# A decoder block on one core: x transposed before the third weight piece, the last batch's norms by token half, its natural scores on four strips

## The reference, cut to what matters

```
A:  qkv = bitlinear(x)            # x rounded to 8 bits per token, weights replaced by their sign
    local softmax over 16 heads of one token; + q @ kv_state of the first 128 tokens
    x1 = layernorm(x + bitlinear(rmsnorm(out)))
B:  q = [ctx, x1] @ Wq ; two key/value sources, one from ctx and one from x1, 32 heads of 16
    scores + alibi, only the last 64 keys ("window"), softmax over both sources
    x2 = layernorm(x1 + att @ Wo)
C:  router over 8 experts, the best two, LoRA weights scaled by them
    y = layernorm(x2 + x2 @ base_w.T + b + lora)
```

## Time and profile before

| | |
|---|---|
| time, median of 3 runs (lowest, highest) | 913.03 us (912.97, 913.53) |
| the profiled execution's own time | 913.3 us |
| its span, first to last instruction | 911.2 us |
| PE, busy share | 802.1 us, 88% |
| DVE | 509.5 us, 56% |
| ACT | 326.4 us, 36% |
| POOL | 85.5 us, 9% |

### The profile page before, as it was taken

The page is one execution under the profiler, slowest core; times in us unless marked ns, Lnnn a source line. Parts: engine busy times, 40 slices in busy tenths (PEclk is TensorE's granted clock), DMA queues, the critical chain, the costliest instruction groups (busy, mean ns, idle before and its releaser), DMA issues.

```text
span 911.2 us, 22548 instructions
## 1 busy us (share of the span) xinstructions
PE 802.1 (88%) x10161; PEld 524.5 (58%) x10209; DVE 509.5 (56%) x1060; ACT 326.4 (36%) x424; POOL 85.5 (9%) x103
## 2 busy tenths in 40 slices
PE   3788878888998989988998989988998979999996
PEld 2466763477445864577445864577445864486443
DVE  4756584448745593748745593648745582435143
ACT  5534224333245224433245224433245124310422
POOL 1111011000300021000300021000300010010001
PEclk9989999999999999999999999999999999997998
DMA  9921000100002000010002000010001000000000
GB/s 345 246 55 47 2 2 1 47 2 2 2 1 70 3 2 1 26 47 2 1 1 71 3 2 1 27 46 1 1 1 48 2 1 1 24 1 1 1 24 23
DMA packets 19022, 27.10 MB, mean 30 GB/s; under 512 B 5608, under 2 KB 7784, under 8 KB 18928
## 3 DMA queue, kind: packets, MB, share of 16 engines
q1 hardware_dynamic: 18784, 25.64, 9.1%
q10 hardware_dynamic: 144, 0.03, 0.0%
HBM read 21.47 MB, written 4.19 MB: 28 GB/s over the span
## 4 chain that ended last, share of the span: by engine, by line
PE 63%; DVE 19%; ACT 12%; issue 4%; POOL 1%; DMA 1%; ACTq 0%; POOLq 0%; SPq 0%; DVEq 0%
ACT p_b L761 7%; PE ps L1148 7%; PE ps L1184 6%; PE ps L1065 6%; PE ps L1225 6%; DVE max_b L1487 6%; PE ps L1113 4%; PE ps L1048 3%; PE ps L1085 3%; PE ps L893 2%; DVE max_a L1385 2%; PE ps L968 2%; PE ps L1173 2%; PE ps L1157 2%; PE ps L978 2%
## 5 line engine op out<-in xcount | busy, mean ns | idle before, releaser
L761 ACT ACTIVATE p_b<-ps 128x2048 f32<-128x2048 f32 x64 | 106.5, 1664 | 115.9 <-PE ps L1157 115.9
L1487 DVE TENSOR_REDUCE max_b<-ps 128x4 f32<-128x768 f32 (+2 forms) x160 | 106.6, 711 | 31.1 <-PE ps L1127 19.3
L1363 DVE SCALAR_TENSOR_TENSOR nat<-ps,st_a,qkv_bias 128x512 f32<-128x512 f32 x48 | 35.7, 744 | 98.0 <-PE ps L893 96.8
L1113 PE MATMUL ps<-qk_b 32*128 32x192 f32 (+2 forms) x1024 | 65.5, 341 | 22.9 <-DVE max_b L1487 16.8
L1148 PE MATMUL ps<-qk_b 32*128 32x512 f32 (+1 forms) x512 | 66.2, 586 | 9.7 <-ACT p_b L761 5.2
L1113 PEld LDWEIGHTS ps<-qk_b 32*128 32x128 f32 x1024 | 46.2, 188 | 39.9 <-DVE max_b L1487 27.3
L1225 PE MATMUL ps<-base_t,x_t 128*128 128x512 f32 x128 | 63.8, 624 | 0.0
L1173 PE MATMUL ps<-p_b,v_b 128*32 128x256 f32 (+1 forms) x1024 | 61.7, 358 | 2.4 <-ACT p_b L761 2.0
L1048 PE MATMUL ps<-c_t,wq 128*128 128x256 f32 x256 | 60.6, 385 | 2.4 <-DVE out_a L1408 2.3
L1065 PE MATMUL ps<-x_t,wq 128*128 128x256 f32 x256 | 61.3, 385 | 0.0
L1184 PE MATMUL ps<-wo,o_fb 128*128 128x512 f32 x128 | 59.0, 599 | 0.8 <-DVE o_fb L1529 0.8
(11 more groups left out here) (207 smaller groups left out, 1432.7 us busy)
## 6 DMA issues: line engine op xcount, KB each, us to landing
x_in<-x SPq DMA_DIRECT2D x8, 512.0 KB, 5.4
p_b<-ctx SPq DMA_DIRECT2D x8, 512.0 KB, 4.6
y<-x SPq DMA_DIRECT2D x7, 512.0 KB, 3.3
p_b<-L_attn_qkv_w SPq DMA_DIRECT2D x2, 1024.0 KB, 6.5
p_b<-L_xattn_Wq SPq DMA_DIRECT2D x1, 2048.0 KB, 14.9
x<-L_attn_qkv_w SPq DMA_DIRECT2D x2, 512.0 KB, 9.5
x<-L_ffn_base_w SPq DMA_DIRECT2D x2, 512.0 KB, 10.2
wo<-L_xattn_Wo SPq DMA_DIRECT2D x8, 128.0 KB, 9.1
```

The lines of the kernel that those rows point to most:

```text
L761: act.activation(p_b[:, j % 2, :, 0:cols], ps[:, 4:8, 0:cols], ACT.Exp, scale=DB ** -0.5).then_inc(pb_here.sem, 1)
L1113: pe.matmul(bank(4 + r)[:, (i % 2) * N:(i % 2) * N + 2 * n * S], q_b[strip[r], i, :, :].rearrange("p h q -> p (h q)"), k_b[strip[r], half, ...
L1363: dve.scalar_tensor_tensor(nat[:, t, w, :], bank(nat_bank(b, w)), st_a[:, 2, t:t + 1], qkv_bias[:, w * C:(w + 1) * C], ALU.mult, ALU.add). ...
L1487: ins = dve.tensor_reduce(max_b[:, half, 0, i:i + k, 2 * n:2 * n + 2], ps[:, 4 + 2 * n:6 + 2 * n, :].rearrange("p r (i n) -> p i r n", i=2 ...
```

## The change

What is the same for all batches: in `b2`, the scores of the even query block on strips 0 and 1 are issued after DVE's first report of the pair before, those on strips 2 and 3 after the second, then the odd block's on all four; slopes and masks go to strips 0 and 1 for both blocks, and then to strips 2 and 3.

```
+                if pair:
+                    sb_max(pe, b, 8 * half + 2 * pair - 1)
+                scores(even, first)
+                if pair:
                     sb_max(pe, b, 8 * half + 2 * pair)
...
+                scores(even, second)
+                scores(odd, first)
+                scores(odd, second)
+                for strips in (first, second):
+                    slope(even, strips)
+                    slope(odd, strips)
+                    masks(even, strips)
+                    masks(odd, strips)
```

```
             def b2(b, half, pair):
-                alone = isinstance(b, int) and b == NB - 1
+                keep_on(b, NB - 1, (0, 0, 6, 6, 4, 4, 2, 2)[4 * half + pair])
...
             def c1_x2(b, t):
-                    keep_on(b, NB - 1, 2 if t else 14)
+                    keep_on(b, NB - 1, 4)
                     x2_here(pe, b, t + 1)
-                    if t:
+                    if alone(b):
+                        pb_here(pe, b)
+                    elif t:
...
             def c1(b, t):
                 keep_on(b, NB - 1, 2)
-                x2t_here(pe, b)
+                if alone(b):
+                    outa_here(pe, b)
+                x2t_here(pe, b, t + 1 if alone(b) else None)
...
+            def half_stats(c, b, t, z, mv, rs, row, here):
+                c.start(dve, b, 2 * t)
+                c.link(dve.bn_stats(stats[:, t, :], z[:, t, :]))
+                c.link(dve.bn_aggr(mv[:, t, :], stats[:, t, :]))
+                dve.tensor_scalar(rs[:, row, t:t + 1], mv[:, t, 1:2], EPS_LN, None, ALU.add).then_inc(here.sem, 1)
+
+            def half_shift(b, t, mv, rs, row, rstd, done):
+                rstd(dve, b, t + 1)
+                dve.scalar_tensor_tensor(rs[:, row + 2, t:t + 1], mv[:, t, 0:1], -1.0, rs[:, row + 1, t:t + 1], ALU.mult, ALU.mult).then_inc(done.sem, 1)
```

```
+            def warm(n):
+                for _ in range(n):
+                    pe.matmul(bank(7).rearrange("p (a n) -> p a n", a=4), eyeb, eyeb.unsqueeze(1).to_broadcast([P, 4, P]), start=True, stop=True)
+
             for n in range(2):
+                warm((22, 3)[n])
                 pe.wait_ge(signed.sem, n + 1)
                 sign_turn(n)
...
             def early(b):
+                warm(3)
...
             def a1(b):
+                if isinstance(b, int) and b == 0:
+                    warm(11)
...
-            first = [(0, late), (1, mix), (0, b1), (1, a0), (2, a0), (1, b1)]
+            first = [(0, late), (0, b1), (1, b1), (1, a0), (2, a0), (1, mix)]
...
-            first = [(-1, early), (0, a1), (0, of(a1_qkv, 0, [0])), (0, of(a1_qkv, 0, [1])), (0, of(a1_qkv, 0, [2])), (0, of(a1_qkv, 1, [0])),
+            first = [(0, a1), (-1, early), (0, of(a1_qkv, 0, [0])), (0, of(a1_qkv, 0, [1])), (0, of(a1_qkv, 0, [2])), (0, of(a1_qkv, 1, [0])),
```

More of the change, by code:

```diff
@@ L411, in program, with alone @@
         NEXT, A, B, C_, D_ = -1, 0, 1, 2, 3
+        def alone(b):
+            return isinstance(b, int) and b == NB - 1
         def apart(b, t):
@@ L575, in b4 @@
             def b4(b):
+                if alone(b):
+                    for t in range(T):
+                        vb_here(pool, b, t + 1)
+                        pool.tensor_tensor(rs_b[:, 1, t:t + 1], rs_b[:, 0, t:t + 1], neghalf[:, 0:1], ALU.pow).then_inc(rb_here.sem, 1)
+                    return
                 vb_here(pool, b)
@@ L1100, in b2 @@
                         v_here(pe, b)
-                        if not alone:
+                        if not (isinstance(b, int) and b + 1 >= NB):
                             ct_here(pe, b + 1)
-                elif not alone:
-                    sb_max(pe, b, 8 * half + 2 * pair)
-                seen = [(i, slice(max(i - 2, 0), i + 1)) for i in (2 * pair, 2 * pair + 1)]
-                o = lambda r, i, n: bank(4 + r)[:, (i % 2) * N:(i % 2) * N + 2 * n * S].rearrange("p (c k) -> p c k", c=n)
@@ new lines, in b2, with scores @@
+                cols = lambda i: slice((i % 2) * N, (i % 2) * N + 2 * S * (min(i, 2) + 1))
+                keys = lambda i: slice(max(i - 2, 0), i + 1)
+                first, second = range(2), range(2, 4)
+                def scores(i, strips):
+                    for r in strips:
+                        pe.matmul(bank(4 + r)[:, cols(i)], q_b[strip[r], i, :, :].rearrange("p h q -> p (h q)"),
+                                  k_b[strip[r], half, keys(i), :, :].rearrange("p c s k -> p (c s k)"),
+                                  start=(i % 2 == 0), stop=False, skip_group_check=True)
@@ new lines, in slope, with masks @@
+                def slope(i, strips):
+                    for r in strips:
+                        at = slice(r * S, r * S + 3)
+                        pe.matmul(bank(4 + r)[:, cols(i)], slopes[at, half, :], places[at, keys(i), :], start=False, stop=False, skip_group_check=True)
+                def masks(i, strips):
+                    for r in strips:
+                        o = bank(4 + r)[:, cols(i)].rearrange("p (c k) -> p c k", c=min(i, 2) + 1)
+                        if i < 2:
+                            mm = pe.matmul(o[:, i, :], rep[strip[r], :], mask_nat[strip[r], 1, :], start=False, stop=True, skip_group_check=True)
+                        else:
+                            mm = pe.matmul(o[:, 0:3:2, :], rep[strip[r], :], mask_nat[strip[r], :, :], start=False, stop=True, skip_group_check=True)
+                        if i % 2 and r % 2:
+                            mm.then_inc(sb_full.sem, 1)
```

202 lines of the change are left out of this document (100 added, 102 removed).

## The result

The changed kernel took 904.2 us (903.5 to 905.2, 4 runs) where the one before took 913.0 in the same comparison (911.2 to 913.5): ratio 0.9894, interval 0.9874 to 0.9914. The chain has the same shape, but TensorE waits far less for VectorE's maxima in the natural scores. The page's chain after, then the views of waits before (L1113 is the scores' product) and after (L1130): us in total, times, longest.

The account below looks back on a forecast made before the run. PE was taken as the main bound, with 63% of the chain of waits. Terms -4.3 -0.5 +2.4 -0.8 -0.5 -2.6 -3.1 sum to -9.4 from 913.3, giving 904.0 us after adjustment; 8-in-10 range 899.5 to 910.5.

Parts of the forecast that it names:

- the +2.4 of the body: Body's natural scores: two-strip groups cost 0.46 us in each of five iterations, rounded up to +2.4.
- Start-up: 22 identity products raise PE's clock and x is transposed before the third weight piece: -4.3 us at batch 0's last block.
- The rival with the signs held up: Start-up: the 22 products delay the sign transposes, gaining 1 instead of 4.3 us; 907.3 us, chance 0.13.
- Slopes and masks of strips 0 and 1, then of 2 and 3, no longer share the array four at a time: Natural scores, batches 0 to 6: the second group of slopes and masks costs 0.23 us a pair, 0.14 in pairs 0 and 4.
- Batches 0 and 6: Natural scores where DVE and PE alternate: about five pairs on the path save 0.15 us each, -0.8 in all.
- Batch 7's scores: Natural scores on four strips with identity products: the low clock goes and maxima are transposed earlier, -2.6 us.
- The +4.2: Batch 7's scores at full clock: period 2.97 against 2.25 on two strips, six pairs losing 0.7 us each.
- The end: Batch 7's last norms by halves: -2.6 us up to the router, -0.5 in the last norm, -3.1 in all.
- (1): Rival: the clock falls in batch 7's scores all the same, -2.6 becoming +2.4; 908.9 us, chance 0.15.
- (2): Rival: two-strip groups are paid in full in all 56 pairs, +12.9 instead of +1.6; 915.2 us, chance 0.11.
- (3): Rival: the 22 start-up products hold up the signs, gaining 1 instead of 4.3 us; 907.3 us, chance 0.13.
- (4): Rival: reorderings of `first` and `last` bring 3 us more than seen; 901 us, chance 0.11.

Follow-up runs that it names:

- e6: Changed kernel without its 39 start-up identity products, x still transposed ahead of the third weight piece; 902.5 us.
- e2: Changed kernel with 3, 4, 3 and 4 identity products ahead of the pairs of batch 0's second half of natural scores; 904.4 us.
- e1: Changed kernel with natural scores of batches 0 to 6 on four strips as before, batch 7 keeping two-strip groups; 906.6 us.
- e3: Changed kernel with batch 7's two last layer norms taken over both token halves at once, as before; 910.0 us.
- e5: Changed kernel run again with no edit, to see differences between executions; 903.1 us.
- e9: Changed kernel with 12 start-up identity products for 22, batch 7's scores two strips at a time again, no products ahead of its pairs; 909.6 us.
- e12: Changed kernel with 12 start-up identity products for 22, plus 4 at 38 us in TensorE's wait for ACT's maxima copy; 898.8 us.
- e4: Changed kernel without the 24 identity products ahead of batch 7's pairs of natural scores; 907.6 us.
- e10: As e9, but with 16 identity products ahead of batch 7's two-strip groups; 909.3 us.
- e11: Changed kernel with 12 start-up identity products for 22, batch 6's last base quarter back behind batch 7's first transposed scores; 903.2 us.

## Why the prediction was right, and where it was not

904.0 was said and 904.2 measured. The direction and the large terms were right, but that the sum fits this well is luck, since its errors cancel: the +2.4 of the body did not come, the start-up and batch 7's transposed scores gained 1.9 more than was said, the end 0.7 more, and against them stood 3.5 in batch 0 that was not foreseen and about 1.8 of small gains that failed.

**Start-up: mechanism right.** The 22 products ended at 9.8 for the 10.7 said, the signs took the 1.06 for 1.0, the products started at 18.04 for 18.9, DVE at 19.18 for 19.9. e6 shows the part of the order, 18.91, as worked out (-2.4). The rival with the signs held up is not another case but the tail of this one: with a late landing of the constants (e2, 11.85) 2.4 of the 5.1 are left at the `kc` copy; 1.8 of the loss is there at the `q_t` copy, 0.9 goes with the low stretch near 40. The step missing was the one behind: I ended the account at 35.84, while the low stretch near 40, which every profile has, took 10.2 us in e1, e2, e3, e5 and e9, 3.4 in e12 and 6.8 in the others, before too (there at 46.0).

**"Slopes and masks of strips 0 and 1, then of 2 and 3, no longer share the array four at a time": this step failed.** 0.46 per iteration was said, 0.00 came (after and e1, both). I took two packs from batch 7 of before, where the second pair of strips waited for DVE or held 16 float32 scores of its own, and let the array work in program order. In the records of a pair that doesn't wait all eight slopes start ahead of the first mask, so the order is not that of the program; that it is kept within each strip fits, but the records don't name strips. Eight slopes take 0.35 for 0.34. In the pairs that wait the groups do come apart, by 0.3, but that time is covered by the earlier start of strips 0 and 1. The Trainium skill (TensorE: Matmul & The Clock Gate, "Measured speedup vs the span model") gives a pack one matmul's time plus some 4 ns for each further tile; taken per group in the program it said +3.5 for the body, and the trace disagrees with that use of it, with 1.15 for 1.14 a pair: where nothing waits, tiles of two groups form one pack. (By the section's own terms 0.39 in place of 0.23 would give 0.24, 0.17, 0.24 and 0.39 an iteration, 5.2 in all and not 3.5; and five times 0.46 is 2.3.) The 12.9 us of waits that vanished from the list were cover all the same: PE starts two strips of the even block early and then waits for the second report in the middle of the pair, where the masks end as before.

**Batches 0 and 6: right in size for one half of batch 6, and given back.** In batch 6's second half the masks of pairs 5, 6 and 7 end 1.55, 1.76 and 1.97 ahead of before: 0.2 a period for the 0.15 said, and e1 shows 0.44 for the half. The maxima's transposes stand 2.07 ahead, but ACT now copies those of `a3_t` first (747.09), and the maxima's copy is 1.60 ahead. Another 0.5 had gone by the first half's copy (734.62 to 733.09, 1.53 ahead, for 2.04 in the body); e1, with the old form, lost 0.3 there and e5 0.25, so it belongs to the order of `last` and to the execution rather than to the form. In batch 0 nothing was gained at full clock either (e5, 0.27 more than before): pair 6's masks end another 0.2 ahead, pair 7's 0.95 less, with both `a3` stages now in front of it. That batch 0's scores could lose the clock was in no part of the prediction: it was looked for in batch 7 alone.

**Batch 7's scores: right,** -2.55 for -2.6, and by the mechanism said. At 2.94 a period is slower than on two strips (2.25), but the clock stays up with the products; it fell without them (e4), and in one half of two with the other form (e9, e10). The +4.2 was too large at full clock: by e9 the other form would bring 0.56 in the half that could be compared, since a base quarter fits into the longer wait and not into the shorter.

**The end: right in kind, 0.7 short in size.** -3.8 for -3.1. The missing part is in the last norm: besides the 0.76 of ACT's second half, POOL's pow on one column takes 0.55 for 0.70, and the aggregation of one half 0.18 for 0.25.

**Not foreseen: -1.06 in batch 7's transposed scores,** from the quarter moved into the scores' last wait (e11).

Of the rivals, (1), the clock falling in batch 7, is what the products prevent (e4); (2), two-strip groups paid in full, is refuted by e1. (3) came true in part in some executions, see the start-up. (4) did not come: the stretches that hold mainly reorderings, to batch 0's first maxima and from its second to batch 1's first, gained 0.05 and 0.35. The two gains of 0.5 from orders alone, ahead of batch 0's maxima and at batch 7's entry, gave 0.05 each; where they went is open. No run took the new place of the 13 loads by itself.

## What to carry to other kernels

Filling waits with identity products pays only up to the moment the real work is ready: size the fill by the earliest time of what it stands in front of (12 products gave 900.1 us, none 902.5, 22 903.1; where their constants landed at 4.7, the 22 ended 3.7 after the signs were ready). Compare a stretch, not a total, when executions differ by more than the effect, and profile the same kernel twice before giving a stretch a cause: the one large loss in the table (3.5 us) belonged to one execution. Tiles on different row strips of TensorE overlapped here across groups that the program lists one behind the other, as long as no wait stood between them: read this from the records before pricing an order. And a wait that vanishes is a gain only if what stood behind it moves.

## What the runs showed of the hardware

- Matmuls of 32-row tiles can start out of the program's order: in batch 4's pair 7 eight slopes start from 543.893 to 544.004, all ahead of the first mask (544.061), with four masks listed ahead of the last four slopes.
- The granted clock fell in the same program in different places from one execution to the next (126.2 to 136.5 in one profile of the changed kernel, not in e5), which alone is 3.2 us of 902.
- The same small load, the first constants, landed at 3.11 (e4) to 4.86 us (e10) after the start.
- A low stretch lasts for different times in executions of one program: near 40 us, 6.8 in after, 10.2 in e5.
- In the start-up the same 22 products took 6.26 us (e4) to 7.58 us (e5), with the granted clock's rise at 5.9 and 8.6.
